# Mean-embedding projection on one core: the first mean's chain reordered, with seven extra products into an idle bank

## The reference

```python
valid = sequence_ids < emb_table.shape[0]
safe_ids = jnp.where(valid, sequence_ids, 0)
seq_emb = emb_table[safe_ids] * valid[..., None]
denom = jnp.maximum(valid.sum(axis=1, keepdims=True), 1.0)
user_repr = seq_emb.sum(axis=1) / denom
logits = user_repr @ proj_w + proj_b          # 1024 x 12500
```

## Time and profile before

| what | value |
|---|---|
| median of 3 runs | 640.26 us (637.78 to 640.47) |
| the profiled execution | 639.96 us, of which 638.1 us are the span |
| mean granted TensorE clock | 0.997 of full speed |
| TensorE busy | 609.2 us, 95% |
| VectorE busy | 407.6 us, 64% |
| GpSimd busy | 231.1 us, 36% |
| ScalarE busy | 145.6 us, 23% |
| mean DMA rate | 248 GB/s; in most slices up to 100 us above 340 |

### The profile page before, as it was taken

The page is one execution under the profiler, slowest core; times in us unless marked ns, Lnnn a source line. Parts: engine busy times, 40 slices in busy tenths (PEclk is TensorE's granted clock), DMA queues, the critical chain, the costliest instruction groups (busy, mean ns, idle before and its releaser), DMA issues.

```text
span 638.1 us, 7597 instructions
## 1 busy us (share of the span) xinstructions
PE 609.2 (95%) x2602; PEld 477.3 (75%) x2602; DVE 407.6 (64%) x723; ACT 145.6 (23%) x161; POOL 231.1 (36%) x227
## 2 busy tenths in 40 slices
PE   1989889989999999999999999999999999999997
PEld 0337558768788787788888888888888888888886
DVE  7988949899878898697885554332333333344442
ACT  8917425132122131300200221111011111211210
POOL 5777877777763767566550000000000000000000
PEclk9998999999999999999999999999999999999999
DMA  9979999999997999798893398454555555566632
GB/s 310 387 257 342 385 394 344 358 303 324 315 302 267 311 302 315 238 325 248 253 339 114 99 293 283 123 168 163 173 167 174 177 178 177 175 191 202 218 127 103
DMA packets 77704, 158.31 MB, mean 248 GB/s; under 512 B 9288, under 2 KB 65043, under 8 KB 77659
## 3 DMA queue, kind: packets, MB, share of 16 engines
q1 hardware_dynamic: 60378, 110.30, 51.1%
q0 software_dynamic: 17280, 47.47, 22.9%
HBM read 115.70 MB, written 51.20 MB: 262 GB/s over the span
## 4 chain that ended last, share of the span: by engine, by line
PE 72%; DVE 19%; issue 5%; DMA 2%; DVEq 1%; ACT 0%; POOL 0%; POOLq 0%
PE acc L842 70%; DVE sums L561 7%; DVE w_lo L625 5%; DMA rows<-in_L_rec_emb_table_dram,index 2%; DVE key L518 1%; DVE top L514 1%; DVE stage L640 1%; PE acc L847 1%; DVEq L259 1%; DVE index L516 0%; PE turned L763 0%; PE turned L783 0%; DVE mean L607 0%; DMA ids_sb<-in_r_sequence_ids_dram 0%; DVE key L502 0%
## 5 line engine op out<-in xcount | busy, mean ns | idle before, releaser
L353 POOL DMA_INDIRECT rows<-in_L_rec_emb_table_dram,index x208 | 221.6, 1066 | 96.3 <-issue 55.8
L842 PE MATMUL acc<-w_hi,mean_hi 128*128 128x500 f32 x800 | 225.3, 403 | 0.8 <-ACT mean_hi L438 0.8
L640 DVE TENSOR_TENSOR stage<-acc,bias_sb 128x500 f32<-128x500 f32 x162 | 109.3, 676 | 179.2 <-PE acc L842 179.1
L842 PE MATMUL acc<-w_lo,mean_hi 128*128 128x500 f32 x800 | 214.6, 390 | 0.0
L842 PE MATMUL acc<-w_hi,mean_lo 128*128 128x500 f32 x800 | 213.7, 389 | 0.4 <-DVE mean_lo L612 0.3
L842 PEld LDWEIGHTS acc<-w_hi,mean_hi 128*128 128x128 f32 x800 | 150.7, 190 | 32.0 <-issue 4.3
L842 PEld LDWEIGHTS acc<-w_lo,mean_hi 128*128 128x128 f32 x800 | 150.8, 189 | 31.5
L842 PEld LDWEIGHTS acc<-w_hi,mean_lo 128*128 128x128 f32 x800 | 150.3, 188 | 32.1 <-DVE mean_lo L612 1.2
L561 DVE SCALAR_TENSOR_TENSOR sums<-rows,mask,sums 128x512 f32<-128x512 f32 x165 | 124.0, 752 | 16.2 <-issue 8.2
L422 ACT ACTIVATE w_hi<-w_raw 128x2000 fp32r<-128x2000 f32 x39 | 72.9, 1875 | 235.3 <-PE acc L842 215.8
L625 DVE TENSOR_TENSOR w_lo<-w_raw,w_hi 128x1000 fp32r<-128x1000 f32 x74 | 85.3, 1194 | 13.6 <-ACT w_hi L422 13.6
(11 more groups left out here) (106 smaller groups left out, 193.1 us busy)
## 6 DMA issues: line engine op xcount, KB each, us to landing
out_dram<-stage SPq DMA_DIRECT2D x200, 250.0 KB, 3.9
w_raw<-in_L_rec_proj_w_dram SPq DMA_DIRECT2D x39, 1000.0 KB, 6.6
bias_sb<-in_L_rec_proj_b_dram SPq DMA_DIRECT2D x39, 250.0 KB, 4.9
raw_at_hi<-in_L_rec_proj_w_dram SPq DMA_DIRECT2D x4, 1000.0 KB, 11.6
rows<-in_L_rec_emb_table_dram,index POOLq DMA_INDIRECT x208, 6.0
raw_at_lo<-in_L_rec_proj_w_dram SPq DMA_DIRECT2D x3, 1000.0 KB, 15.2
stage<-in_L_rec_proj_w_dram SPq DMA_DIRECT2D x1, 1000.0 KB, 26.1
ids_sb<-in_r_sequence_ids_dram SPq DMA_DIRECT2D x1, 700.0 KB, 4.4
```

Source lines behind the costliest of these rows:

```text
L353: return pool.indirect_dma_start(out=dst, out_offset=None, in_=table, in_offset=bass.IndirectOffsetOnAxis(ap=column, axis=0), bounds_check ...
L640: dve.tensor_tensor(stage[:, g % STAGE, r - stores[g][0]], acc[:, r % BANKS, 0:BW], bias_sb[:, i % BIAS], ALU.add).then_inc(s_moved_by_dve, 1)
L842: last = nc.tensor.matmul(bank, first, second, start=part + k == 0, stop=part == 2 and k == K - 1 and not by_act[r])
```

## The change

Six edits, all around the first mean:

1. The first tile's packed rows are added before column 14, not 18 (`REST_FIRST_AT`).
2. The second tile's list is made before column 17, not 21 (`LIST_FIRST_AT`).
3. The scaling of `sums` to `rest_mean` is taken out of `first_mean` and stands ahead of `w_low(3)`.
4. Of the third tile's five sorting rounds two stay ahead of the first mean; three stand behind `mean_low(0)`.
5. Four products of 128x500 are put behind column 25 and ahead of `turn(0)`, into bank 4 of `acc`, behind a wait for the fourth low half. Nothing reads them; unit 4 overwrites the bank.
6. Three more such products stand behind `turn(0)`.

```diff
+    SORTED_FIRST = 2
-    FURTHER_BEHIND, LIST_FIRST_AT, BIAS_DUE = 20, 21, 3
+    FURTHER_BEHIND, LIST_FIRST_AT, BIAS_DUE = 20, 17, 3
-    LATE_LOAD, REST_FIRST_AT, OPENED = 7, 18, SPLIT - 1
+    LATE_LOAD, REST_FIRST_AT, OPENED = 7, 14, SPLIT - 1
...
+            def first_further_share():
+
+                dve.tensor_scalar(rest_mean[:], sums[:], inv_count[:, 0:1], None, ALU.mult).then_inc(s_further_mean, 1)
+
             def first_mean():
 
-                dve.tensor_scalar(rest_mean[:], sums[:], inv_count[:, 0:1], None, ALU.mult).then_inc(s_further_mean, 1)
                 dve.wait_ge(s_further_mean, 1)
...
             sum_further(0)
+            first_further_share()
             w_low(3)
-            for r in range(ROUNDS):
+            for r in range(SORTED_FIRST):
                 sort(2, r)
             first_mean()
             mean_low(0)
+            for r in range(SORTED_FIRST, ROUNDS):
+                sort(2, r)
             for c in range(FAST, FAST + 4):
                 add_column(c)
...
+            def keep_clock(times):
+
+                for _ in range(times):
+                    nc.tensor.matmul(acc[:, SPLIT - 1, 0:BW], w_hi[:, 0, 0, 0:P], w_hi[:, 0, 0], start=True, stop=True)
+
...
+            pe.wait_ge(s_w_lo, OPENED)
+            keep_clock(4)
             turn(0)
+            keep_clock(3)
```

## The result

The changed kernel is slower: a median of 640.47 us over 19 runs (639.58 to 642.33) against 638.93 us over 19 runs of the kernel before (637.39 to 640.47). The ratio is 1.0028, its 95% interval 1.0020 to 1.0037: some 1.5 to 1.8 us lost. It is less than the 0.5% that I called the limit of telling, but with 19 runs on each side it is clear of their scatter. I had forecast a small gain, 639.3 us.

The account below looks back on a forecast made before the run. Bound by a wait chain through the second tile's last gather (landed 86.43) into 280 us of unbroken products. Sum 639.96 - 0.9 = 639.1, softened to -0.7: 639.3 us; central case 638.3 to 640.2, range 636.9 to 641.9.

Parts of the forecast that it names:

- Column 25 unmoved by packed rows and list: First tile's columns on TensorE: the last still ends at 45.57 us, since gathers set its time; effect 0.
- The first mean 0.64 us earlier, unit 0 1.38 us shorter: Around the first mean: it starts at 45.6, not 46.26; unit 0 at full clock takes 2.95 us, not 4.33.
- The 2.0 us of units 0 to 7 turn into idle time: TensorE before the second tile's columns: the earlier end of unit 7 becomes idle time at 72 to 78 us; 0 gained.
- The rounds push everything behind them by 1.7 us: VectorE and ScalarE after the first mean's low half: low halves, block 10's load and diagonals (77.7) come 1.7 us late.
- The clock falls ahead of the columns: TensorE before the second tile's columns: after 5.6 us idle the clock falls, low for 3.5 us of work.
- The last gather 1.0 us earlier: Second tile's gathers on GpSimd: stretching by low halves is 4.0 us, not 5.0; bounds -3 to +2 us.
- So the end is 86.7, not 87.6: -0.9: Second tile's columns on TensorE: two at 1.7 us, six at 0.86 from 78.1; -0.9 us, bounds -1.1 to +0.8.
- Rival B: At 72 to 90 us the clock falls ahead of the second tile's columns and stays low; up to 645.6 us; chance 0.12.

Follow-up runs that it names:

- All but edit 4: The changed kernel with all five sorting rounds ahead of the first mean again; ratio 1.0008 to the kernel before, 639.80 us against 639.15.
- The order alone: The kernel before with the packed rows, list, scaling and three rounds moved, without the seven products; ratio 1.0037 to the kernel before, 640.53 us.
- The rounds in VectorE's idle time: The changed kernel with the three rounds moved on behind the second tile's last VectorE column; ratio 0.9993 to the kernel before, 639.01 us.
- The gap filled: The changed kernel with 24 more products ahead of the second tile's columns, into unit 8's idle bank; ratio 1.0014 to the kernel before, 639.47 us.
- Early diagonals: The changed kernel with the second tile's first four diagonals ahead of the rounding of block 10; ratio 1.0004 to the kernel before, 639.35 us.
- The same on edit 4 alone: The kernel before with three rounds moved behind the first mean's low half, plus the second tile's first four diagonals made early; ratio 1.0011 to the kernel before.
- Edit 4 alone: The kernel before with only the three sorting rounds moved behind the first mean's low half; ratio 1.0031 to the kernel before, 641.45 us.
- The products alone: The kernel before with only the seven products added, order untouched; ratio 1.0007 to the kernel before, 638.75 us.
- That with its gap filled: The changed kernel with the three rounds behind the second tile's last VectorE column, plus 15 products ahead of its TensorE columns; ratio 1.0014 to the kernel before, 639.38 us.

## Why the prediction failed, point by point

- **Column 25 unmoved by packed rows and list:** right. It ended at 45.57 (41.01 + 4.56), as before. *All but edit 4* shows no cost of both edits that can be told.
- **The first mean 0.64 us earlier, unit 0 1.38 us shorter:** right. 45.70 and not 46.26; 2.84 us and not 4.33. The clock stayed at full from 45 to 74 us. That the seven products kept it up is likely, not shown: in *The order alone* it stayed up without them.
- **The 2.0 us of units 0 to 7 turn into idle time:** right, and shown by *The rounds in VectorE's idle time*.
- **The rounds push everything behind them by 1.7 us:** right in kind, 2.0 measured: low half of block 4 at 55.44 (55.2 said), diagonals at 77.85 (77.7), idle time 5.76 us (5.6).
- **The clock falls ahead of the columns:** right. Full clock returned at 82 us, 3.6 us after the columns began.
- **The last gather 1.0 us earlier:** the direction was right, 0.4 us was measured. The stretching came to 4.1 us, as said (4.0); but GpSimd began the gather that I had at 54.63 at 54.76, and stood idle for 0.45 and 0.46 us before two later ones, where I had taken 0.30 for all. The gather at 77.75 began inside the low half at 77.66 and took 1.98 us, as the pattern has it. The Trainium skill, "SBUF — State Buffer", section "Who interferes with whom", has the two SBUF inputs as the cause; no run here took that cause away by itself.
- **"So the end is 86.7, not 87.6: -0.9" is the step that failed.** It had two faults. The 86.7 was 87.30: 0.6 us more, since the diagonals began 0.15 us and TensorE's first column 0.3 us later than said, and the low clock lasted somewhat longer. And the 87.6 was not what the kernel before usually does. Its second profile ends these columns at 86.97 and its medians in five sets of runs lie between 638.4 and 639.2 us, so that the first profile (639.96) was slow by about 1 us. Against 86.97 the term is +0.3, not -0.9. With both put right the sum is 638.9 + 0.3 = 639.2 us, and 640.47 was measured: the cost of the later diagonals was not all in the end of these columns. I had compared the profiled execution with a median of three runs, 0.3 us above it, which was itself 1.3 us above the median of the 19.
- **What the sum left out:** the move of unit 7 stands behind the diagonals on ScalarE. It came 2.2 us late and held GpSimd for 1.13 us. I had counted GpSimd's waits for the buffers that VectorE frees, and not this one. From the second mean to the end of the span took 550.1 us instead of 549.6 and 549.4 in the two profiles of before. That this wait makes the difference is not shown, and two profiles speak against it. In *The gap filled* and *Early diagonals* GpSimd was held longer (1.78 and 1.53 us; 1.77 and 1.30), so that the gather which the changed kernel issues at 86.24 came at 86.89 and 86.66, and yet the third mean was earlier: 127.97 and 128.10 instead of 129.31 us. So what costs time behind the second mean stays open, and with it the 0.1% that stays in *The same on edit 4 alone*.
- **Rival B was about half of the mechanism.** I had its place (72 to 90 us) and its price (1.7 us for a column), and gave it 0.12 as I took the low clock to end after 3.5 us of work each time. In the changed kernel's profile that held (3.7 us from the first column on); in *Edit 4 alone* it was 5.9 us, until about 85.2. The other half, late diagonals that cost time at full clock too, no rival had. Four of the changed kernel's 19 runs had a mean clock of 0.992 instead of 0.995 to 0.997, and took 641.4 to 642.3 us.

So, in one line: three sorting rounds ahead of a chain that goes VectorE, SP's load, ScalarE's rounding, diagonals, made TensorE's columns start 4 us later than their first gathers allowed. That this chain carries the loss is shown: it goes when the three rounds move away (0.9993, 1.0008) and when the diagonals alone are made early (1.0004). Its two parts are estimates: about 0.14% with the clock kept up, and as much again by the low clock that the longer idle time brought (changed kernel 1.0028, gap filled 1.0014). The intervals of these ratios are 0.0008 to 0.0011 wide to each side, so the halves are rough, and by what way the first half reaches the end was not found.

## What to carry to other kernels

Before moving work behind a wait, follow what stands behind it on every queue to the next point where two engines meet; here the 2 us surfaced 25 us later, on an engine that the moved work never touched. Take the baseline of a sum that is to be right to 1 us from several executions: one profile was off by 1 us, the larger part of the effect. Work that only keeps the clock up can move the fall to a later gap, and then helps only if that gap is off the path.

## What the hardware showed that I had not expected

How much low clock a run gets differs from one execution of a kernel to the next: the timed runs' mean clocks lie between 0.989 and 1.000, most at 1.000, 0.997, 0.995 or 0.992. In one set of 29 runs of the kernel before, 14 at 0.997 average 638.2 us and three at 0.992 average 639.7; but in another set of 17 (that of *The same on edit 4 alone*) five at 0.997 and three at 0.992 both average 638.7. Where it falls seems to decide what it costs: in unit 0 nothing that can be told (*The products alone*), in the last columns 1.3 us, if all six slower runs of *That with its gap filled* had it where the profile has it. In the profiles of *Edit 4 alone*, *All but edit 4*, *Early diagonals* and *The rounds in VectorE's idle time*, all of one session, the clock also fell between 125 and 137 us, about the third mean. From there to the fourth mean took 40.7 to 41.5 us in these four and 39.7 to 40.3 in the other ten profiles. From the eighth mean to the end is 285.5 to 285.6 us in all 14, so every difference here arises before it. And the low clock can last though TensorE is busy without a break, as the rows of *Edit 4 alone* show up to 84 us and beyond. The Trainium skill, "TensorE: Matmul & The Clock Gate", section "Why this matters for your kernels", asks for no idle gaps between bursts of products; the trace agrees where the gap of 5.76 us was. The traces add that much shorter gaps can stand ahead of a fall (1.49 and 0.78 us), and need not bring one: in *The order alone* none came after 0.94 and 0.78 us.
